# Eight stages on one core: patch work moved between two attentions, gates chosen in four groups, keys and values projected ahead of a norm

## The chip, the cores and the metric

One core of a Trainium2 chip runs the whole kernel. The metric is the device time of one execution in microseconds (us). The engines are PE (TensorE, matmuls), DVE (VectorE), ACT (ScalarE), POOL (GpSimd) and SP (SyncE, which only issues transfers here). They run side by side, each in the order of its own program, and wait for one another by semaphores.

## The reference, cut to what matters

x has 4 batches of 256 rows of 128 (1024 rows). Each stage normalises x and adds its result to it. Four of the eight stages are touched.

```python
x = x + _L0_xattn_ref(...)   # masked attention, 8 heads of 16
x = x + _L0_ffn_ref(...)     # 4 rounds of routed experts
x = x + _L1_xattn_ref(...)   # unmasked attention, 16 heads of 8, context keys too
x = x + _L1_ffn_ref(...)     # gated attention: 8 heads, 8 experts per head
x = x + _L2_xattn_ref(...)   # patch attention
x = x + _L2_ffn_ref(...)     # dense experts
x = x + _L3_xattn_ref(...)   # attention with a null key, 16 heads of 64
x = x + _L3_ffn_ref(...)     # sparse experts

# in _L1_ffn_ref: for values (v) and outputs (o), per row and head, 2 of 8 experts
probs = jax.nn.sigmoid(raw)                       # [B, S, H=8, E=8]
vals, idx = jax.lax.top_k(probs, K)
vals = vals / jnp.clip(vals.sum(-1, keepdims=True), 1e-09) * route_scale
gate = (jax.nn.one_hot(idx, E) * vals[..., None]).sum(-2)

# in _L2_xattn_ref: a decayed running sum over the normalised context, read at boundaries
bidx = jnp.cumsum(patch_lens, axis=1) - 1
boundary_mask = boundary_mask.at[jnp.arange(bsz)[:, None], bidx].set(1)
_, s = jax.lax.associative_scan(comb, (a_b, u), axis=1)
plug = jnp.clip(jnp.cumsum(boundary_mask, axis=1) - 1, 0, plen - 1)
depool_out = depool[jnp.arange(bsz)[:, None], plug]

# in _L3_xattn_ref: queries come from x, keys and values from the context
q = einsum(x, Wq);  k, v = split(einsum(context, Wkv))
k = concatenate((null_k, k));  v = concatenate((null_v, v))
attn = softmax(q * scale @ k.T);  out = layernorm((attn @ v) @ Wout)
```

## The kernel before

Every stage is five Python functions, one per engine, and each engine runs its functions of all stages in a row. x, the normalised `xn`, its transpose `xnT`, the context and its transpose `ctxT` stay in SBUF. The order of work is the order in which the code is written. Between stages the engines are tied by `x_tiles`, a semaphore that DVE raises for each finished tile of x. The `Norm` class makes the norm: statistics on DVE (L80 to L93), a power on POOL (L133), scaling on DVE (L123), eight transposes on PE (L140), and two copies on ACT (L148).

**The attentions (`packed_attention`).** The same function makes stage 0 (masked) and stage 2 (unmasked). Queries and keys are projected, split into three bf16 parts by ACT and DVE (L497, L751, L501, L756), stored to DRAM by SP and ACT (L317) and loaded back in another layout by SP (L652, L662). Then one loop runs over i: a first pass (L365) finds each row's maximum on DVE (L787), the maxima go through a transpose (L422), ACT, DVE or POOL, and a transfer (L721) back into the queries, and some steps later (`LAG`) a second pass (L379), exponentials on ACT (L545) and weighted values (L409) follow. In the masked stage `values` (L351, L774, L778) makes the values of a batch, and the transpose of L422 waits for them.

**The patch work (`PatchAhead`).** The part of patch attention that doesn't depend on x is made early, in the masked attention. The pieces are, in order: `pe_ends`, `dve_hits`, `dve_statistics`, `pe_counts` (L1914), `dve_bounds`, `pe_plugs` (L1927, 8 matmuls), `act_decays` (two Relu L1937, two Exp L1940), `dve_rows` (L1954), `dve_keep` (L1962), `pe_sums` (L1971) and `dve_take` (L1980). Those from `pe_counts` on stand inside the masked loop at i = 0 to 4. PE waits at s = 1 for the last of them (`z_ready`), and POOL waits for it before it splits the weights of the next stage (L1436, L1438).

**The gated attention.** For head h the values are eight experts' products (`experts`, L1554), merged by ACT (L1620), DVE (L1725) and POOL. The gates are chosen by DVE in `select` (L1692 to L1708): 14 operations over rows x heads x experts and 4 narrow ones. It runs four times, each over four heads: side 0 (values) of heads 0 to 3 ahead of everything, side 1 (outputs) of heads 0 to 3 behind the maxima of head 0, and the same for heads 4 to 7 behind the maxima of heads 1 and 2. PE's queries and keys for a head are L1541, the scores L1568, the weighted values L1591; the maxima are L1757.

**The null-key attention.** PE does the transposes of the norm, then the null values times the output weights (L2108), waits until DVE has copied them (L2254), and then projects the first pair of heads in the order q, k, q, k, v, v (L2123, L2126, L2131) through two PSUM banks. Then come the scores (L2148).

## Time and profile before

| | |
|---|---|
| median of 3 runs (lowest, highest) | 1276.37 us (1274.05, 1276.74) |
| the profiled execution: its own time, its span | 1281.73 us, 1280.1 us |
| share of the chain that ended last: PE, DVE, ACT | 68%, 13%, 8% |
| busy: PE, DVE, ACT, POOL | 87%, 61%, 53%, 31% |
| mean granted TensorE clock | 0.908 |
| HBM traffic over the span | 34 GB/s |

The span is counted from the first instruction; 1.6 us of the time lie outside it. The granted clock is a share of 2.4 GHz: 1.00 is 2.4 and 0.50 is 1.2 GHz. By the first and last instruction of each stage the span divides into masked attention 0 to 122 us, rounds to 350, unmasked attention to 523, gated attention to 853, patch attention to 875, dense experts to 1003, null-key attention to 1213, and sparse experts to 1280. PE does most of the chain, but at the start of most stages it is DVE, ACT, POOL and transfers that hold it, and these are the places that the change touches.

### The profile page before, as it was taken

To read this page: it belongs to the slowest core of one execution; us is meant where nothing else is said; L and a number is where in the kernel's file an instruction comes from. 1 tells how busy PE (TensorE), PEld (TensorE's weight loads), DVE (VectorE), ACT (ScalarE), POOL (GpSimd) and SP (SyncE) were. 2 spreads that over 40 slices of the span, in tenths; PEclk is the share of its full clock that TensorE was granted. 3 is DMA by queue.
4 is the path that set the end of the run, shared out by engine and by line. 5 is a ranking of instruction groups with operands and counts; after the bars stand their busy time and mean duration, and the time that the engine had idled before them with its cause. 6 is when DMAs were issued, how large, how long until landed. Compare 5 with 4: busy or idle time off the path is not lost.

```text
span 1280.1 us, 18272 instructions
## 1 busy us (share of the span) xinstructions
PE 1111.4 (87%) x6234; PEld 773.2 (60%) x6234; DVE 781.1 (61%) x1914; ACT 683.4 (53%) x1613; POOL 395.9 (31%) x612
## 2 busy tenths in 40 slices
PE   3677899999859998778899999967999799998777
PEld 2346677777613344656677777745777567675665
DVE  5754687788667672668766677664111366666464
ACT  3253567666515575366677778752343266666022
POOL 5311112111121110236466676672000144444200
PEclk8686899999966799888989999986999899999979
DMA  5411000000050400300000000214000100000000
GB/s 208 100 49 58 1 1 13 1 1 1 1 161 20 170 21 2 132 0 1 1 1 1 1 1 17 116 46 192 1 1 1 67 1 1 1 2 2 1 1 17
DMA packets 26572, 45.10 MB, mean 35 GB/s; under 512 B 3536, under 2 KB 23792, under 8 KB 25200
## 3 DMA queue, kind: packets, MB, share of 16 engines
q1 hardware_dynamic: 23936, 41.57, 9.4%
q10 hardware_dynamic: 2544, 2.36, 0.6%
q8 instruction: 50, 0.82, 0.3%
q14 instruction: 42, 0.34, 0.1%
HBM read 36.94 MB, written 6.82 MB: 34 GB/s over the span
## 4 chain that ended last, share of the span: by engine, by line
PE 68%; DVE 13%; ACT 8%; issue 5%; POOL 2%; DMA 2%; SPq 2%; ACTq 0%; DVEq 0%; POOLq 0%
PE psum L1179 7%; PE psum L1554 7%; PE psum L1169 5%; PE psum L919 5%; PE psum L929 4%; ACT region_d L1620 3%; PE psum L2187 3%; PE psum L409 2%; PE psum L2164 2%; PE psum L2131 2%; PE psum L2148 2%; PE psum L2126 2%; PE psum L1541 2%; PE psum L365 2%; PE psum L1591 2%
## 5 line engine op out<-in xcount | busy, mean ns | idle before, releaser
L1554 PE MATMUL psum<-gated_parts 128*128 128x512 f32 x768 | 198.6, 413 | 16.6 <-DVE region_d L1725 14.7
L1554 PEld LDWEIGHTS psum<-gated_parts 128*128 128x128 f32 x768 | 142.5, 193 | 68.5 <-DVE region_d L1725 32.6
L1794 POOL TENSOR_TENSOR region_d<-region_d 128x256 f32<-128x256 f32 x128 | 101.9, 796 | 121.4 <-DVE region_d L1725 120.1
L1254 ACT ACTIVATE rounds_work<-psum,region_c 128x512 f32<-128x512 f32 x128 | 87.0, 689 | 59.3 <-PE psum L1169 59.2
L787 DVE TENSOR_REDUCE work<-psum 128x1 f32<-128x512 f32 x128 | 82.1, 686 | 34.4 <-PE psum L365 32.8
L1725 DVE SCALAR_TENSOR_TENSOR region_d<-psum,ctx,region_d 128x128 f32<-128x128 f32 x256 | 71.8, 343 | 45.3 <-ACT region_d L1620 41.7
L1620 ACT ACTIVATE region_d<-psum,gated_work 128x128 f32<-128x128 f32 x256 | 75.2, 438 | 44.9 <-issue 26.1
L1179 PE MATMUL psum<-parts,split 128*128 128x512 f32 x384 | 97.6, 404 | 0.0
L1169 PE MATMUL psum<-parts,split 128*128 128x512 f32 x384 | 94.2, 396 | 0.0
L1324 DVE TENSOR_TENSOR parts<-rounds_work,parts 128x1024 fp32r<-128x1024 f32 x64 | 77.5, 1223 | 20.1 <-POOL parts L1410 17.4
L1725 DVE SCALAR_TENSOR_TENSOR region_d<-psum,gated_work,region_d 128x128 f32<-128x128 f32 x256 | 71.3, 344 | 29.1 <-ACT region_d L1620 19.0
L1410 POOL CAST parts<-rounds_work 128x1024 fp32r<-128x1024 f32 x32 | 33.3, 1042 | 179.6 <-ACT rounds_work L1254 179.6
L2215 ACT ACTIVATE null_work<-psum,null_work 128x257 f32<-128x257 f32 x128 | 59.7, 472 | 45.6 <-DVE null_work L2258 45.6
L1169 PEld LDWEIGHTS psum<-parts,split 128*128 128x128 f32 x384 | 73.4, 192 | 15.6 <-issue 0.2
L1179 PEld LDWEIGHTS psum<-parts,split 128*128 128x128 f32 x384 | 70.8, 191 | 19.6 <-issue 6.1
L545 ACT ACTIVATE work<-psum 128x1024 f32<-128x1024 f32 x64 | 65.1, 1024 | 30.5 <-PE psum L379 28.3
L1620 ACT ACTIVATE region_d<-psum,ctx 128x128 f32<-128x128 f32 x256 | 73.7, 385 | 13.8 <-PE psum L1554 12.5
L991 ACT ACTIVATE work_behind<-psum,region_e 128x512 f32<-128x512 f32 x64 | 44.0, 687 | 65.9 <-PE psum L919 64.3
L365 PE MATMUL psum<-work 48*128 48x512 bf16 x128 | 56.3, 481 | 13.6 <-DMA work<-q_parts 10.5
L2258 DVE TENSOR_REDUCE null_work<-psum 128x2 f32<-128x514 f32 x64 | 44.0, 688 | 37.7 <-PE psum L2148 37.7
L1064 DVE SCALAR_TENSOR_TENSOR xn<-psum,work_behind,xn 128x128 f32<-128x128 f32 x64 | 18.0, 344 | 79.9 <-PE psum L929 79.8
L2346 POOL TENSOR_TENSOR null_work<-null_work 128x512 f32<-128x512 f32 x64 | 66.5, 1039 | 0.0
(377 smaller groups left out, 2263.3 us busy)
## 6 DMA issues: line engine op xcount, KB each, us to landing
region_a<-in_l1v SPq DMA_DIRECT2D x1, 4096.0 KB, 15.4
region_b_last<-in_l1o SPq DMA_DIRECT2D x1, 4096.0 KB, 12.4
region_a<-in_l2f SPq DMA_DIRECT2D x1, 4096.0 KB, 13.4
region_b_last<-in_l3f_small SPq DMA_DIRECT2D x1, 4096.0 KB, 19.7
region_a<-in_l3f SPq DMA_DIRECT2D x1, 2080.0 KB, 7.6
region_c<-in_l0f SPq DMA_DIRECT2D x1, 2076.0 KB, 12.3
region_c<-in_l3x SPq DMA_DIRECT2D x1, 2048.0 KB, 8.0
ctx_parts<-front_work SPq DMA_DIRECT2D x6, 256.0 KB, 3.6
```

The lines of the kernel that those rows point to most:

```text
L365: ins = pe.matmul(bank[g % 2][:, j * NK:(j + 1) * NK], QS[b % BUFS][rows_at(side, R_MAX), slot, t * P:(t + 1) * P], KS[b % BUFS][rows_at(s ...
L545: act.activation(PT[s % 2].rearrange("p (a n) -> p a n", a=2), k.pair(2 + 2 * (s % 2)), ACT.Exp, scale=scale).then_inc(p2_exp.semaphore, 1)
L787: dve.tensor_reduce(NM[:, b, heads[0]:heads[0] + HPG, t], bank[g % 2][:, :].rearrange("p (j n) -> p j n", j=HPG), AX.X, ALU.max, negate=Tr ...
L1169: ins = pe.matmul(bank[f], w1_part[a][:, e, f * P:(f + 1) * P], cur_part[b][:, half_of(s % 2)], start=n == 0, stop=n == len(PASSES) - 1)
L1179: ins = pe.matmul(bank[4 + g % 2], w2_part[a][:, g % E, f, :], hidden_part[b][g % 2][:, f, :], start=f == 0 and n == 0, stop=f == FT - 1 a ...
L1254: act.activation(H[g % 2][:, f, :], bank[f], ACT.Gelu_apprx_tanh, bias=W("b1")[:, (g % E) * FT + f:(g % E) * FT + f + 1]).then_inc(h_ready ...
L1324: dve.tensor_tensor(two(hidden_part[1][g % 2], c), two(H[g % 2], c), two(hidden_part[0][g % 2], c).bitcast(F32), ALU.subtract).then_inc(h_ ...
L1554: ins = pe.matmul(bank[2 * (n % 2) + c], src[a][:, t * P:(t + 1) * P], weights[b][:, piece(c)], start=m == 0, stop=m == len(PASSES) - 1)
L1620: ins = act.activation(scaled[n % RING][:, e, :], bank[2 * (n % 2)][:, e * P:(e + 1) * P], ACT.Copy, scale=scalars[:, n % NT, e:e + 1])
L1725: ins = dve.scalar_tensor_tensor(out=tile, in0=bank[2 * (n % 2) + 1][:, e * P:(e + 1) * P], scalar=scalars[:, n % NT, HALF_E + e:HALF_E + ...
L1794: pool.tensor_tensor(tile[:, 0:2, :], tile[:, 0:2, :], tile[:, 2:4, :], ALU.add).then_inc(k.pool_chain, 1)
L2346: pool.tensor_tensor(PR[g % 4][:, :, 0:S], PR[g % 4][:, :, 0:S], r.broadcast_to([P, TPB, S]), ALU.mult)\
```

## The change

Four edits. (1) `pe_plugs`, `act_decays`, `dve_rows`, `dve_keep`, `pe_sums` and `dve_take` leave the masked attention for the front of the unmasked one; `pe_counts` and `dve_bounds` stay in the masked stage, ahead of its loop. What the late pieces need (`upto16`, `before`, `least`, `bound`) lies in a new SBUF tensor, `patch_kept`. (2) POOL's split of the next stage's weights waits for the first exponential instead of `z_ready`. (3) `select` runs eight times, over head groups of 1, 3, 2 and 2. (4) In the null-key attention the first pair's chunks go in the order k, k, v, v, q, q, three of them ahead of the norm's transposes and in banks of their own, and L2108 comes last.

```diff
@@ packed_attention, tensor @@
         if masked:
             ahead.pe_ends(pe)
+        else:
+            pe.wait_ge(k.x_tiles, NT * number)
+            ahead.pe_plugs(pe)
         k.norm.tensor(pe, use, k.xn)
...
         if masked:
             pe.wait_ge(*biased.at(4))
+            ahead.pe_counts(pe)
         else:
             pe.wait_ge(*rest.at(first_of(3)))
             pe.wait_ge(*part.at(first_of(3)))
+            ahead.pe_sums(pe)
...
-                if masked and s == 1:
-                    pe.wait_ge(ahead.z_ready, 2)
+                if s == 1:
+                    pe.wait_ge(*((ahead.bound_ready, 1) if masked else (ahead.z_ready, 2)))
...
-            if masked and i == 0:
-                ahead.pe_counts(pe)
-            if masked and i == 1:
-                ahead.pe_plugs(pe)
-            if masked and i == 3:
-                ahead.pe_sums(pe)
@@ scalar, gpsimd, vector @@
+        if not masked:
+            ahead.act_decays(act)
         k.norm.scalar(act, use, k.xnT)
...
-            if masked and i == 1:
-                ahead.act_decays(act)
...
-            pool.wait_ge(ahead.z_ready, 2)
+            pool.wait_ge(*p2_exp.at(1))
             split.gpsimd(pool)
...
+            if pair == 0 and not masked:
+                ahead.dve_rows(dve, chain)
+                ahead.dve_keep(dve)
         if masked:
             ahead.dve_hits(dve, chain)
             ahead.dve_statistics(dve, chain)
+            ahead.dve_bounds(dve)
+        else:
+            ahead.dve_take(dve)
@@ gated_attention @@
+    GATE_GROUPS = (slice(0, 1), slice(1, 4), slice(4, 6), slice(6, 8))
...
-                if h % (NH // 2) == 0:
-                    act.wait_ge(gates_ready, 1 if h == 0 else 3)
+                for i, heads in enumerate(GATE_GROUPS):
+                    if h == heads.start:
+                        act.wait_ge(gates_ready, 2 * i + 1)
...
             if h < NH:
+                if h == 1:
+                    select(2)
+                elif 1 < h < 6:
+                    select(h + 2)
                 merge_block(values_block(h), gates[:, :, 0, h, :])
                 if h > 0:
                     maxima(h)
                 if h == 0:
-                    select(1, first_heads)
-                elif h < 3:
-                    select(h - 1, last_heads)
+                    select(1)
+                elif h == 1:
+                    select(3)
@@ null_key_attention @@
+    FIRST = (1, 3, 4, 5, 0, 2)
...
+    def chunk(p, i):
+
+        n, c = len(CHUNKS) * p + i, FIRST[i] if p == 0 else i
+        return n, c, c // 2 % 2 if c < 4 else c - 4, k.bank[1 + i] if n < 2 else k.bank[6 + n % 2]
...
-        for c in range(len(CHUNKS)):
-            project(0, c)
+        for i in range(3):
+            project(0, i)
+        k.norm.tensor(pe, use, k.xn, banks=(4, 5))
+        project(0, 3)
+        for i in range(4, 6):
+            pe.wait_ge(k.norm.T_ready, 2 * use + i - 3)
+            project(0, i)
+        for p in range(PAIRS):
+            ins = pe.matmul(bank[5][0:HEADS, 0:D], W("nv")[:, p, :], W("o")[:, p, :], start=p == 0, stop=p == PAIRS - 1)
+        ins.then_inc(nvw_psum, 1)
         pe.wait_ge(null_ready, 4)
         scores(0, 0)
+        pe.wait_ge(nvw_sb, 1)
```

Three places of the order, before and after. ACT at the front of the unmasked attention, before (`parts` and `rounds_work` belong to the stage ahead):

```order
L1265 ACTIVATE rounds_work<-psum 128x512 x2
L148 ACTIVATE xnT<-psum 128x512 x2
L497 ACTIVATE work<-psum 128x512 x2
L501 ACTIVATE work<-work 128x512 x2
L317 DMA q_parts<-work 16x8x512 x6
```

The same place on ACT after the change:

```order
L1265 ACTIVATE rounds_work<-psum 128x512 x2
L1945 ACTIVATE work<-psum,patch_kept 128x1024 x2
L1948 ACT_TABLE_LOAD
L1948 ACTIVATE work<-work 128x1024 x2
L148 ACTIVATE xnT<-psum 128x512 x2
L500 ACTIVATE work<-psum 128x512 x2
L504 ACTIVATE work<-work 128x512 x2
L319 DMA q_parts<-work 16x8x512 x6
```

Two Relu and two Exp of 1024 columns stand ahead of the copies of the transposes, and the load of the Exp table, which stood at L545 behind the first maxima, is now among them. DVE at the same front after the change:

```order
L752 TENSOR_TENSOR work<-psum,work 128x512 x2
L757 TENSOR_TENSOR work<-work 128x512 x2
L1960 TENSOR_SCALAR ctx_rstd<-ctx_rstd 128x8
L1962 SCALAR_TENSOR_TENSOR work<-ctx,ctx_rstd,region_e 128x128 x8
L1970 SCALAR_TENSOR_TENSOR work<-psum,patch_kept,work 128x1024 x2
L752 TENSOR_TENSOR work<-psum,work 128x512 x2
L757 TENSOR_TENSOR work<-work 128x512 x2
L1988 TENSOR_TENSOR mask_bc<-psum,region_e 128x512 x2
```

The two halves of the splitting, which stood side by side, now have 11 instructions between them. PE at the front of the null-key attention, before:

```order
L929 MATMUL psum<-region_a,work_behind 128x128 x32
L140 MATMUL psum<-ident,xn 128x128 x8
L2108 MATMUL psum<-region_d 16x128 x8
L2123 MATMUL psum<-xnT,region_d 128x512
L2126 MATMUL psum<-ctxT,region_c 128x512 x2
L2123 MATMUL psum<-xnT,region_d 128x512
L2126 MATMUL psum<-ctxT,region_c 128x512 x2
L2131 MATMUL psum<-region_c,ctxT 128x128 x16
L2148 MATMUL psum<-null_parts 128x258 x24
```

And after:

```order
L929 MATMUL psum<-region_a,work_behind 128x128 x32
L2138 MATMUL psum<-ctxT,region_c 128x512 x4
L2143 MATMUL psum<-region_c,ctxT 128x128 x8
L140 MATMUL psum<-ident,xn 128x128 x8
L2143 MATMUL psum<-region_c,ctxT 128x128 x8
L2135 MATMUL psum<-xnT,region_d 128x512 x2
L2188 MATMUL psum<-region_d 16x128 x8
L2160 MATMUL psum<-null_parts 128x258 x24
```

Both keys and half of the values stand between the last matmuls of the stage ahead and the transposes, and only one half of the values, the queries and the null values are left behind them.

## Rows read from the trace of the kernel before

**Rows 1.** Timeline, masked attention: start us, us, instruction, [idle before <- releaser].
```profile
37.08 2.19 DVE L1954 SCALAR_TENSOR_TENSOR front_work<-ctx,ctx_rstd,region_e 128x128 f32<-128x128 f32 x8
...
39.30 2.12 ACT L1937 ACTIVATE front_work<-psum,front_work 128x1024 f32<-128x1024 f32 x2 [12.22 <-PE psum L1927]
...
43.70 2.45 DVE L1962 SCALAR_TENSOR_TENSOR front_work<-psum,front_work 128x1024 f32<-128x1024 f32 x2
...
44.89 21.62 SPq L721 DMA_DIRECT2D front_work<-front_work  x10
...
46.20 5.22 PE L1971 MATMUL psum<-front_work 128*128 128x128 f32 x32 [3.48 <-DVE front_work L1962]
...
55.53 2.41 POOL L1438 TENSOR_TENSOR split<-region_c,split 128x1024 fp32r<-128x1024 f32 x1
...
56.11 2.90 DVE L778 TENSOR_SCALAR front_work<-front_work,mask_col 128x128 f32<-128x128 f32 x2
...
59.16 0.27 PE L422 MATMUL psum<-ident,front_work 128*8 128x128 f32 x1 [3.76 <-DVE front_work L778]
...
71.09 0.48 DVE L778 TENSOR_SCALAR front_work<-front_work,mask_col 128x128 f32<-128x128 f32 x2
...
93.32 2.08 PE L351 MATMUL psum<-region_d,ctxT 128*128 128x128 f32 x8
```

**Rows 2.** Timeline, front of the unmasked attention.
```profile
354.27 0.60 ACT L148 ACTIVATE xnT<-psum 128x512 f32<-128x512 f32 x1 [9.82 <-PE psum L140]
...
363.62 1.29 DVE L751 TENSOR_TENSOR work<-psum,work 128x512 f32<-128x512 f32 x2 [3.19 <-ACT work L497]
...
369.90 0.61 PE L365 MATMUL psum<-work 48*128 48x512 bf16 x2 [10.50 <-DMA work<-q_parts]
...
388.28 1.28 ACT L545 ACT_TABLE_LOAD   x1
389.57 1.94 ACT L545 ACTIVATE work<-psum 128x1024 f32<-128x1024 f32 x2
```

**Rows 3.** Windows: stretch, us, busy (instructions) by engine, granted clock, DMA.
```profile
388.00:394.00 6.00, 5.43 (x37) 1.78 (x35) 3.87 (x6) 4.51 (x5) 0.00 (x0) 0.50 0.00 0
```

**Rows 4.** Timeline of PE and DVE, gated attention.
```profile
537.03 3.72 PE L1568 MATMUL psum<-gated_work 128*128 128x256 f32 x16 [0.69 <-ACT gated_work L1647]
...
565.53 6.58 PE L1541 MATMUL psum<-xnT,region_d 128*128 128x512 f32 x8 [3.47 <-DVE gated_parts L1741]
...
609.04 3.72 PE L1591 MATMUL psum<-region_c,gated_work 128*128 128x256 f32 x16
...
653.20 3.71 PE L1591 MATMUL psum<-region_c,gated_work 128*128 128x256 f32 x16
...
689.93 3.72 PE L1591 MATMUL psum<-region_c,gated_work 128*128 128x256 f32 x16
...
556.55 0.41 DVE L1692 TENSOR_REDUCE gated_work<-ctx 128x32 f32<-128x256 f32 x1
...
564.92 0.22 DVE L1749 TENSOR_TENSOR gated_work<-ctx,gated_work 128x64 f32<-128x64 f32 x1
...
574.09 1.13 DVE L1725 SCALAR_TENSOR_TENSOR region_d<-psum,ctx,region_d 128x128 f32<-128x128 f32 x4 [7.62 <-ACT region_d L1620]
...
662.33 1.12 DVE L1725 SCALAR_TENSOR_TENSOR region_d<-psum,ctx,region_d 128x128 f32<-128x128 f32 x4 [4.53 <-ACT region_d L1620]
```

**Rows 5.** Timeline of PE, front of the null-key attention.
```profile
1007.06 2.50 PE L140 MATMUL psum<-ident,xn 128*128 128x128 f32 x8 [5.71 <-DVE xn L123]
...
1009.49 2.98 PE L2108 MATMUL psum<-region_d 128*16 128x128 f32 x16
...
1012.93 1.10 PE L2123 MATMUL psum<-xnT,region_d 128*128 128x512 f32 x2 [0.46 <-DVE null_work L2254]
...
1019.04 3.73 PE L2131 MATMUL psum<-region_c,ctxT 128*128 128x128 f32 x32
...
1022.70 0.98 PE L2148 MATMUL psum<-null_parts 64*128 64x258 f32 x12
```

More of the change, by code:

```diff
@@ L218, in packed_attention @@
         cp = [k.carve(BF16, T) for _ in range(3)]
+    else:
+        ahead.carve_later()
     q_dram, k_dram = k.q_dram[number], k.k_dram[number]
@@ L795, in vector @@
                     row_maxima(b, n)
-            if masked and i == 0:
-                ahead.dve_bounds(dve)
-                ahead.dve_rows(dve, chain)
             if masked and i % SU == 0 and 0 < i <= ALL:
@@ L810, in vector @@
                                   ALU.subtract).then_inc(nm_rest.semaphore, 1)
-            if masked and i == 2:
-                ahead.dve_keep(dve)
-            if masked and i == 4:
-                ahead.dve_take(dve)
             if masked and i % STEPS == VALUES_AT % STEPS and VALUES_AT <= i < ALL + VALUES_AT:
@@ L1679, in vector, with select @@
         dve.wait_ge(probs_ready, 1)
-        shape = [P, NT, NH // 2, E]
-        falling = W("falling").unsqueeze(1).unsqueeze(1).broadcast_to(shape)
-        def wide(a):
-            return a.unsqueeze(3).broadcast_to(shape)
-        def select(side, heads):
+        def select(n):
+            side, heads = n % 2, GATE_GROUPS[n // 2]
+            shape = [P, NT, heads.stop - heads.start, E]
+            falling = W("falling").unsqueeze(1).unsqueeze(1).broadcast_to(shape)
+            wide = lambda a: a.unsqueeze(3).broadcast_to(shape)
             of = lambda a: a.rearrange("p (t a h) e -> p t a h e", t=NT, a=2)[:, :, side, heads, :]
@@ L1708, in select @@
             dve.tensor_tensor(g, g, wide(c2), ALU.mult).then_inc(gates_ready, 1)
-            dve.wait_ge(gates_ready, side + 2 * (heads.start > 0) + 1)
+            dve.wait_ge(gates_ready, n + 1)
         def low_weights(n, c):
@@ L2229, in projections @@
             ins.then_inc(proj_sb, 1)
-        for c in range(len(CHUNKS)):
-            projections(0, c)
+        for i in range(3):
+            projections(0, i)
+        k.norm.scalar(act, use, k.xnT, banks=(4, 5))
+        for i in range(3, 6):
+            projections(0, i)
         exponentials(0)
```

75 lines of the change are left out of this document (36 added, 39 removed).

## The prediction

> **What bounds the kernel now.** I read the chain that ended last first: PE holds 68% of it. In the middle of every stage PE is full, and a change on another engine is worth nothing there. So I looked, stage by stage, at the first microseconds on the timeline: what stands idle, and whose end it waits for. The four edits touch four such fronts, and I cost each at the instruction of PE or DVE behind which the rest of the stage follows as before.
>
> **Masked attention: what leaves.** In the rows of the loop, PE waits 3.48 us for DVE's L1962, computes the sums for 5.22 us, and reaches the maxima's transpose L422 at 59.16, 3.76 us late, released by DVE's L778 [rows 1]. Leaving are 2.19 us (L1954) and 2.45 us (L1962) on DVE, two pairs of 2.1 us on ACT (L1937 and its Exp), and 5.22 us on PE. Their sum, 14 us, is not the gain, because SP bounds this front too: the first transfer of maxima is issued at 44.89 [rows 1], behind the loads of all batches, and that doesn't move. Three issues and the flight of the last take some 3.6 us (estimate), so the second pass starts at 48.5. Then PE does the second pass, a first pass and the values. It has done little by then and its clock will be low, where the values took 2.08 us [rows 1]; with the passes, 3.3 us, to 51.8. DVE adds the bias (0.4) and runs L778. Before, L778 took 2.90 us with POOL's L1438 of 2.41 us beside it, and 0.48 us once POOL was done [rows 1]. POOL's split now starts after the first exponential, at about 50.5, so it meets L778 again, and I take 2.90 us: 55.1 against 59.16, **-4.0 us**. If L778 escapes it is -6.5; if one more such meeting occurs later, -2. Behind this the loop runs at its old pace. The counts, now ahead of the loop, lie in PE's wait for the loaded queries.
> The 2.4 us that L778 lost fit what the Trainium skill says in "SBUF — State Buffer", on the shared port: DVE and GpSimd lock one port pair for a whole instruction and the second one blocks. By that rule moving POOL's start to the first exponential keeps the collision, which is the case I took; without the rule I would say -6.5.
>
> **Unmasked attention: what comes in.** The plugs fit PE's pause before the transposes and cost nothing; they are ready at about 350.8. ACT then does the Relu pair (2.12 [rows 1]), the table load (1.28 [rows 2]) and the Exp pair (2.0, taken as the Relu pair), to 356.1, where its L148 began at 354.27 [rows 2]: 1.8 us late. All behind it (projection, splitting, q stores, loads) shifts by this, since PE's L365 ends a wait of 10.50 us for the loaded queries at 369.90 [rows 2]; it would start at 371.7. DVE has a pause of 3.19 us ahead of L751 at 363.62 [rows 2], from 360.4, now 362.2. Into it go rows and keep: 2.4 + 2.5 = 4.9 us, to 367.0, then the subtractions L751 (1.3) to 368.3. PE waits for these before the sums; the 5.22 us of the sums [rows 1], again after a long pause, end at 373.5. That is 3.6 us later than 369.90. Back comes the table load of L545 at 388.28 [rows 2], of which I count 0.3, because PE had other work nearly to its end. `dve_take` waits for the sums and delays the first maxima by about 0.1. POOL's fills and the second half of the stores have several us to spare. **+3.3 us.** Bounds: +1.8, if the sums run at the full clock in 3.4 and end before the queries land; +5, if PE starts the projections slower by the low clock as well.
> The Trainium skill ("ScalarE: Activation LUTs", What ACT_TABLE_LOAD costs) adds a drain of about 1.38 us to each load. The trace shows none: the load at 388.28 ends with its 1.28 us and the next ACTIVATE starts at 389.57 [rows 2]. By the page the term would be +4.7, and the total 1260.7.
>
> **Gated attention.** A select over four heads costs 7.5 us: 14 wide operations of 0.41 with a gap of 0.04, and about 1.1 for the narrow ones (from 556.55 to 564.92 it stood 8.4, with a reciprocal and two stretched operations in it) [rows 4]. An operation on 64 columns takes 0.22 [rows 4]. So one head costs 14 x 0.26 + 0.95 = 4.5 us; by interpolation three heads cost 6.5 and two heads 5.5. DVE's total grows from 30 to 44 us, and the place decides.
> - Ahead of head 0 the select ends 3 us earlier, but PE's scores end at 540.75 [rows 4] and the first merge waits for ACT behind them: 0, at most -0.3.
> - Behind head 0: 4.5 in place of 8.1, and PE continues at 562.1 instead of 565.53, up to -3.5 and a warm L1541 in place of 6.58 us [rows 4]. But head 1 waits for its own select: DVE is free at 563.3, ends three heads at 569.8, and ACT starts there instead of just ahead of the merge of 574.09, at 572.85: **-3.0**. PE stands 2.7 us meanwhile; a low clock after this costs up to 2 more. I take +1.
> - Behind the maxima of head 1: 6.5 instead of 7.5, **-1.0**.
> - Head 2 had the last select. From L1591 to L1591 it took 44.16 us, and head 3 took 36.73 [rows 4]: **-7.4**.
> - Heads 2 to 5 now begin with a select of 5.5 in DVE's pause of 4.53 [rows 4]: merges 0.9 late. PE is two tiles ahead of DVE and DVE merges faster than PE multiplies, so PE loses about 0.5 each: **+2**. Bounds 0 and 3.7.
> Together -8.4, taken as **-8.5 us**; from -12 to -5.
>
> **Null-key attention.** PE is idle for 5.71 us before the transposes at 1007.06 [rows 5], from 1001.35. Two keys (each twice a query's 1.10, less when warm) and half of the values (1.9 of the 3.73) [rows 5] fill it nearly: 5.3 to 6.3 us. The last tile of xn sets the end of the transposes, 1009.3. After it come the other half of the values (1.8), two queries (0.9 each) and L2108: 2.98 before [rows 5], half on a low clock, now 1.7 to 2.9. Scores start at 1014.6 to 1015.8 instead of 1022.70 [rows 5]; q's low part is ready at about 1013.4. PE has been busy since 1001, so I take 1014.8: **-7.9 us**; from -9 to -6.
>
> **The sum.** -4.0 + 3.3 - 8.5 - 7.9 = -17.1 us. The profiled execution took 1281.7 (span 1280.1 and 1.6 around it) and would take 1264.6. It is 5.4 above the median of the runs, and none of the four places depends on that, so the forecast is 1276.4 - 17.1 = **1259.3 us**.
>
> **Rivals.**
> - *The sums keep PE warm* in the unmasked stage. From 388 to 394 PE was busy 5.43 of 6 us at a granted clock of 0.50 [rows 3], and stayed so for some eight steps of 2 us. If the 5 us of full matmuls raise the clock and it lasts over 17 us of first passes, these steps end on DVE at about 1.5 us: -3.7 more, 1255.6. For it: after the sums in the masked stage the clock was full. Against: it fell there at the next pause of PE.
> - *The gates bite.* Every late merge costs its full 0.9 us and head 1 leaves PE cold: +1.7 and +1, with the low bound of the masked stage about +2: 1264.
> - *The table switch drains*: 1260.7, as above.
> - *Slower*: PE's pause in heads 1 to 5 is long enough for the clock to fall. L1541 took 6.58 us after 3.47 us of idling [rows 4] and half as much when warm, so each head would cost 3.3 + 0.9. Five of them are 21 us against the 3 in my sum: +18, 1277. It decides from 3.9 us per head on. Against it: the select exceeds the pause by 0.9 us only, and PE kept its clock over its pauses of that length.
> - *The early projections do nothing*, because another engine holds the scores: DVE's low parts or POOL's null keys. Both are done by 1013.4 in my count. If wrong, up to +5, 1264.
>
> **How the numbers follow.** All four terms within their bounds near the middle 0.55; warm sums 0.15; gates or other terms at their weak ends 0.17; the drain 0.05; slower 0.03; something unseen 0.05. The forecast is that of the first. The bounds added in squares give about 5 us down and 5 up; with warm sums below and the weak ends above I give 1250 to 1268. A change below 0.2% (2.6 us) can hardly be measured. Faster by more 0.95, within 0.02, slower 0.03.
>
> **What would show it.** In the new trace: the second pass of the masked stage at 48 to 49 and the first L422 behind the values near 55; L778 again at 2.9; stage 2 starting 4 us earlier; its first L370 3.6 us later from the end of stage 1 than before, behind the sums; ACT's table load at L1948; head 1's first scaling behind the end of a select; head 2 near 37 us instead of 44; no pause of PE ahead of the null-key transposes; 12.5 to 14 us from the last L929 to the first scores, where it was 21.3. I am wrong if pauses of PE and a clock of 0.50 appear at the start of heads 2 to 5, or if the unmasked front grows by more than 5 us.

## The result, and the profile of the changed kernel

| | median us (lowest to highest) | executions | ratio of times, 95% |
|---|---|---|---|
| before | 1276.08 (1273.69 to 1279.12) | 16 | |
| changed | 1269.53 (1263.85 to 1283.76) | 16 | 0.9946 (0.9923 to 0.9969) |

The change made the kernel 6.9 us faster (0.0054 x 1276). The prediction was 1259.3 with a range to 1268, so it was 10 us too low, and the result lies outside the range. The changed kernel's executions also spread over 20 us where those of before spread over 5, and follow the mean granted clock: at 0.919 they took 1264 to 1267, at 0.912 and less 1270 and more. The ratios, here and below, leave out an execution that lies more than 1.5% above the fastest of its kernel (1283.76 here), which the medians keep.

The table shows where the time went, stage by stage, in the two profiled executions (1281.73 and 1275.16 us, each some 5.5 us above the median of its kernel). The ends of the stages are read from first and last starts: PE's first L464 (L465 now), the last matmul of the rounds at L1179, DVE's first L123 of the gated attention and of its successor, L123 of the null-key stage, PE's first L2460 (L2482).

| stage | predicted | before, us | changed, us | difference |
|---|---|---|---|---|
| masked attention | -4.0 | 106.6 | 106.9 | +0.3 |
| rounds | 0 | 239.8 | 238.3 | -1.5 |
| unmasked attention | +3.3 | 176.2 | 184.1 | +7.9 |
| gated attention | -8.5 | 339.2 | 332.0 | -7.2 |
| up to the null-key norm | 0 | 144.9 | 145.4 | +0.5 |
| null-key attention | -7.9 | 211.2 | 204.6 | -6.6 |
| last stages | 0 | 62.2 | 62.2 | 0 |

The two later stages did nearly what was forecast; the two attentions between which the patch work moved did not. First the masked one, timeline of the changed kernel (start us, us, instruction, [idle before <- releaser]); it answers to [rows 1]:
```profile
46.96 42.68 SPq L722 DMA_DIRECT2D front_work<-front_work  x21
...
54.68 1.03 PE L384 MATMUL psum<-front_work 100*128 100x256 bf16 x4 [8.84 <-DMA front_work<-front_work]
...
57.96 2.34 POOL L1438 TENSOR_TENSOR split<-region_c,split 128x1024 fp32r<-128x1024 f32 x1
58.39 2.97 DVE L785 TENSOR_SCALAR front_work<-front_work,mask_col 128x128 f32<-128x128 f32 x2
...
61.51 0.37 PE L427 MATMUL psum<-ident,front_work 128*8 128x128 f32 x1 [3.23 <-DVE front_work L785]
```
The work of the patch attention is gone, yet the transpose behind the values starts at 61.51, later than the 59.16 of [rows 1]. PE stood 8.84 us for a DMA. The prediction had the first transfer of maxima issued at 44.89 as before and the second pass at 48.5; it was issued at 46.96 and the second pass came at 54.68, 7.7 us behind the issue where the prediction had 3.6. L785 beside POOL's split took 2.97 us, as foreseen.

The front of the unmasked attention, which answers to [rows 2]:
```profile
348.67 1.05 PE L1935 MATMUL psum<-patch_kept 128*128 128x256 bf16 x8 [0.85 <-DVE x L1366]
...
349.75 2.12 ACT L1945 ACTIVATE work<-psum,patch_kept 128x1024 f32<-128x1024 f32 x2 [6.51 <-PE psum L1935]
...
351.89 1.28 ACT L1948 ACT_TABLE_LOAD   x1
353.19 2.00 ACT L1948 ACTIVATE work<-work 128x1024 f32<-128x1024 f32 x2
...
355.82 2.04 PE L347 MATMUL psum<-xnT,region_d 128*128 128x512 f32 x2 [1.50 <-ACT xnT L148]
...
362.43 2.19 DVE L1962 SCALAR_TENSOR_TENSOR work<-ctx,ctx_rstd,region_e 128x128 f32<-128x128 f32 x8
364.54 2.46 DVE L1970 SCALAR_TENSOR_TENSOR work<-psum,patch_kept,work 128x1024 f32<-128x1024 f32 x2
366.92 1.27 DVE L752 TENSOR_TENSOR work<-psum,work 128x512 f32<-128x512 f32 x2
...
368.25 6.35 PE L1979 MATMUL psum<-work 128*128 128x128 f32 x32 [6.75 <-DVE work L752]
...
374.53 0.39 PE L370 MATMUL psum<-work 48*128 48x512 bf16 x2
...
377.17 1.20 PE L370 MATMUL psum<-work 48*128 48x512 bf16 x2 [0.21 <-DVE work L794]
```
The order of events is the predicted one: decays on ACT, rows and products on DVE, then the sums, which took 6.35 us for the 5.22 of [rows 1], and the first pass directly behind them.

The gated attention, PE, which answers to [rows 4]. Between the copies of L1592 lie heads 2 and 3:
```profile
569.26 3.70 PE L1542 MATMUL psum<-xnT,region_d 128*128 128x512 f32 x8 [0.39 <-DVE gated_parts L1741]
...
612.84 3.72 PE L1592 MATMUL psum<-region_c,gated_work 128*128 128x256 f32 x16
...
650.32 3.71 PE L1592 MATMUL psum<-region_c,gated_work 128*128 128x256 f32 x16
...
687.75 3.72 PE L1592 MATMUL psum<-region_c,gated_work 128*128 128x256 f32 x16
```
Head 2 takes 37.48 us (44.16 before) and head 3 37.43 (36.73 before). The matmuls of L1542, those of queries and keys, took 3.70 us where they took 6.58.

The front of the null-key attention, PE, which answers to [rows 5]:
```profile
1007.05 1.09 PE L140 MATMUL psum<-ident,xn 128*128 128x128 f32 x4 [0.49 <-DVE xn L123]
1008.30 1.10 PE L140 MATMUL psum<-ident,xn 128*128 128x128 f32 x4 [0.16 <-DVE xn L123]
1009.24 1.95 PE L2143 MATMUL psum<-region_c,ctxT 128*128 128x128 f32 x16
1011.02 2.04 PE L2135 MATMUL psum<-xnT,region_d 128*128 128x512 f32 x4
1012.99 1.92 PE L2188 MATMUL psum<-region_d 128*16 128x128 f32 x16
1014.84 0.98 PE L2160 MATMUL psum<-null_parts 64*128 64x258 f32 x12
1018.67 1.66 PE L2160 MATMUL psum<-null_parts 64*128 64x258 f32 x12 [2.84 <-ACT null_work L2235]
```
The pause of 5.71 us is filled, and the scores start at 1014.84 where the prediction said 1014.8.

### The profile page after: what moved, and what is told of

Its sections match the earlier page's. It is cut to its first block, busy times and chain, and to the rows that moved or that the text cites. A ratio compares the mean times of both kernels' runs of the same rounds, so it can differ in the third digit from the quotient of the medians.

```text
span 1273.5 us, 18344 instructions
## 1 busy us (share of the span) xinstructions
PE 1113.0 (87%) x6234; PEld 772.5 (61%) x6234; DVE 787.3 (62%) x1986; ACT 684.2 (54%) x1613; POOL 395.4 (31%) x612
## 4 chain that ended last, share of the span: by engine, by line
PE 66%; DVE 11%; ACT 9%; issue 5%; SPq 3%; DMA 2%; POOL 2%; ACTq 0%; DVEq 0%; POOLq 0%
PE psum L1179 8%; PE psum L1169 7%; PE psum L1555 6%; PE psum L919 5%; PE psum L929 4%; ACT region_d L1621 4%; PE psum L2208 3%; PE psum L2176 2%; PE psum L2160 2%; PE psum L414 2%; PE psum L2143 2%; ACT region_c L1638 2%; PE psum L1592 2%; PE psum L1569 2%; PE psum L2138 2%
## 5 line engine op out<-in xcount | busy, mean ns | idle before, releaser
L1179 PE MATMUL psum<-parts,split 128*128 128x512 f32 x384 | 99.3, 408 | 0.0
L1169 PE MATMUL psum<-parts,split 128*128 128x512 f32 x384 | 96.7, 402 | 0.0
L1621 ACT ACTIVATE region_d<-psum,ctx 128x128 f32<-128x128 f32 x256 | 73.5, 383 | 20.5 <-PE psum L1555 16.4
L1179 PEld LDWEIGHTS psum<-parts,split 128*128 128x128 f32 x384 | 70.8, 191 | 20.9 <-issue 6.1
L548 ACT ACTIVATE work<-psum 128x1024 f32<-128x1024 f32 x64 | 65.2, 1024 | 34.0 <-PE psum L384 31.9
L929 PEld LDWEIGHTS psum<-region_a,work_behind 128*128 128x128 f32 x512 | 59.5, 192 | 7.2 <-issue 7.2
```

The costliest lines, as they stand in the source:

```text
L548: act.activation(PT[s % 2].rearrange("p (a n) -> p a n", a=2), k.pair(2 + 2 * (s % 2)), ACT.Exp, scale=scale).then_inc(p2_exp.semaphore, 1)
L929: ins = pe.matmul(bank[4 + g % 2][:, t * P:(t + 1) * P], H[g % 2][:, f, t * P:(t + 1) * P], W("w2")[:, i // 2, f, :], start=f == 0, stop=f ...
L1169: ins = pe.matmul(bank[f], w1_part[a][:, e, f * P:(f + 1) * P], cur_part[b][:, half_of(s % 2)], start=n == 0, stop=n == len(PASSES) - 1)
L1179: ins = pe.matmul(bank[4 + g % 2], w2_part[a][:, g % E, f, :], hidden_part[b][g % 2][:, f, :], start=f == 0 and n == 0, stop=f == FT - 1 a ...
L1621: ins = act.activation(scaled[n % RING][:, e, :], bank[2 * (n % 2)][:, e * P:(e + 1) * P], ACT.Copy, scale=scalars[:, n % NT, e:e + 1])
```

## The experiments

### One part at a time

Theory at this point: the missing 10 us belong to the patch move, by some mechanism in the two attentions. Rival: the three parts act on each other. The three parts touch different functions, so each was put alone on the kernel before. Runs e1, e2, e3 and e4, in this order; the edits are the parts of the diff above (e1: `packed_attention`, `PatchAhead` and the memory lines; e2: `gated_attention`; e3: `null_key_attention`; e4: the last two).

> The patch attention's move alone, gates and null-key attention as before. By the steps of the prediction this would be -4.0 in the masked attention and +3.3 in the unmasked one, -0.7 us, so about 1275.4. By the profile of the changed kernel (masked attention +0.3, rounds -1.4, unmasked attention +8.0) it is about +7 us, 1283. Which of the two comes shows whether the missing 10 us of the forecast all belong to this part. A second theory, that the missing time lies in the join of the three parts (gates or null-key stage slowed by the moved memory), wants about 1276 here.

> The gates in four groups alone. Predicted -8.5 us, so 1267.6; the profile of the changed kernel shows -7.2 in that stage, so 1268.9 if the edits don't act on each other. If the parts do act on each other, this one differs from -7.2 by more than 1 us.

> The null-key attention's keys and values ahead of the norm alone. Predicted -7.9 us, so 1268.2; the profile of the changed kernel shows -6.5, so 1269.6.

> Gates and null-key edits, the patch attention left where it was. If the three parts add up and the patch move costs about 7 us: -13.7 by the changed kernel's profile, 1262.4, faster than the changed kernel. If the patch move is worth -0.7 as predicted and the loss is an interaction, this one has about the changed kernel's time, 1270. The spread over executions is looked at too: the changed kernel's runs lie 20 us apart and those of the kernel before 5 us; if the patch move brought the spread, this kernel's runs lie within some 6 us.

| | median us | ratio to before, 95% | as a difference |
|---|---|---|---|
| e1 patch move | 1280.84 | 1.0046 (1.0024 to 1.0068) | +5.9 |
| e2 gates | 1270.15 | 0.9957 (0.9942 to 0.9973) | -5.5 |
| e3 null-key | 1272.77 | 0.9972 (0.996 to 0.9984) | -3.6 |
| e4 gates and null-key | 1264.28 | 0.9907 (0.989 to 0.9925) | -11.9 |

The patch move alone makes the kernel slower by 5.9 us, near the +7 that the profile gave and far from the -0.7 of my sum; without it the kernel is 5 us faster than with it. The gates and the null-key edit alone measure less than in their stages, and together more than their sum. The profiles say where they lose when alone. In e2 the null-key attention, whose code is that of before, took 213.7 us for 211.2: behind a wait of the same length the twelve matmuls of the scores took 1.66 us (e2, first line) where before (second line) took 0.99, and within the next 6 us PE fell 2.5 us behind.
```profile
1013.22 1.66 PE L2152 MATMUL psum<-null_parts 64*128 64x258 f32 x12 [2.75 <-ACT null_work L2219]
```
```profile
1026.43 0.99 PE L2148 MATMUL psum<-null_parts 64*128 64x258 f32 x12 [2.75 <-ACT null_work L2215]
```
In e3 that stage took 207.3 us where e4's took 204.6. The difference arises late, over a stretch of the same work in both: the granted clock was 0.59 from 1172 to 1180 in e3 and 1.00 from 1167 to 1175 in e4. It is one profile of each kernel, so this places the loss in these executions and does not tell how often it comes.

The spread seemed to follow the patch move, since e4's executions lie within 5.2 us and e1's within 14.7. Later runs don't bear that out: e6 and e12, without the move, spread over 16.4 and 14.6 us, and e7, with it, over 4.7.

### What is slow in the masked attention: a start address

The transfer queue of SP, before:
```profile
41.47 1.46 SPq L662 DMA_DIRECT2D front_work<-k_parts  x3
42.98 1.87 SPq L662 DMA_DIRECT2D front_work<-q_parts  x4
```
and changed:
```profile
41.10 3.04 SPq L663 DMA_DIRECT2D front_work<-k_parts  x3
44.18 2.73 SPq L663 DMA_DIRECT2D front_work<-q_parts  x4
```
The same seven loads took 3.3 us of SP before and 5.8 after. The view of the DMA queues over the first 60 us (packets, MB, share of 16 engines) says why. Before:
```profile
q1 hardware_dynamic: 8720, 9.05, 51.9%
```
Changed:
```profile
q1 hardware_dynamic: 8720, 9.05, 65.4%
```
The same packets and bytes took longer, 57 ns for one (0.519 x 60 us x 16 / 8720) against 72. It was 66.6% in e1 and 53.6 to 54.4% in e2, e3 and e4, so it belongs to the patch move. The move adds a tensor `patch_kept` of 264 words ahead of the work area, which so begins 1056 bytes further on. The area holds the slots to which the loads write rows of 256 bf16 numbers, 512 bytes. Theory A: the new start address makes the packets slow. Theory B: what the engines do beside the loads. Four kernels shift nothing but that address.

e5, e7: the changed kernel with 8 and 24 words more (1088 and 1152 bytes).
```
-PATCH_KEPT = S + 2 * TPB + NT // 2
+PATCH_KEPT = S + 2 * TPB + NT // 2 + 8      # e7: + 24
```
e6, e8: the kernel before with an unused tensor of 8 and 32 words (32 and 128 bytes).
```
         self.mask_bias = sb("mask_bias", [1, T], BF16)
+        self.pad = sb("pad", [P, 8])            # e8: 32
...
-WORK = REGION_B + 18090
+WORK = REGION_B + 18090 - 8                     # e8: 32
```


> The changed kernel with 8 words more in the new tensor of kept values, 272 instead of 264, so that the work area behind it starts 1088 bytes later than in the kernel before instead of 1056; nothing else. In both kernels that hold the patch move the DMA packets of the first 60 us take 65 to 67% of the window against 52 to 54% in the four without it, same packets and bytes. Theory A, the shift of the work area by 1056 bytes (32 bytes off a multiple of 64) makes the packets slow: here the share is back to 52 to 54%, the first transfer of maxima is issued at about 43.5 and lands as before, the masked attention ends 2 to 4 us earlier than the changed kernel's 106.9, and the time falls by about 3 us to 1266.5. Theory B, the missing POOL, ACT and DVE work beside the loads or the changed order makes them slow: share 65 to 67% again, 1269.5. The Trainium skill, page DMA: Bandwidth & Descriptors, section How a descriptor splits into AXI transactions, counts from multiples of 256 bytes, and by it this shift would bring nothing.

> The kernel before with an unused tensor of 8 words (32 bytes) ahead of the work area, which is 8 words shorter; not one instruction differs. Theory A: the packets of the first 60 us take about 66%, the masked attention ends some 2 us later (about 107.5), and the time is 2 to 4 us above 1275.9. Theory B: 52 to 54% and no difference.

> The changed kernel with 24 words more in the kept tensor, so that the work area lies 1152 bytes later than before, on a multiple of 256 by my addition of the tensors ahead of it. Theory A: as with 8 words more, 1266.5. If multiples of 256 bytes count, as the same section of the Trainium skill has it, this one is better than the one with 8 words more and its packets take less than 52%.

> The kernel before with an unused tensor of 32 words (128 bytes) ahead of the work area. Theory A: no difference to before (52 to 54%, 1276). If multiples of 256 count: packets below 52% and a gain of 1 to 3 us.

The unused 32 bytes of e6 raised the share from 52 to 65.3%, without one instruction changed, so theory B falls. But so did 128 bytes (e8, 63.1%), and e5 and e7 stayed at 61.1 and 62.3%: so it is not multiples of 64, as I had it in theory A. The times are: e5 1265.50 (0.9891, 0.9857 to 0.9925), e7 1265.40 (0.9903, 0.9877 to 0.9929), e6 1278.35 (1.0007, 0.9984 to 1.003), e8 1279.09 (1.001, 0.9994 to 1.0026). To the kernel before the slow packets cost nothing that can be measured, which refutes the 2 to 4 us that I expected.

In the built program the work area of the kernel before starts at byte 123136, 481 x 256, and none of the shifts so far keeps a multiple of 256; e7 and e8 had been meant as such multiples, by a wrong sum of the tensors ahead of the area. The next four are these: e9 is the changed kernel with `+ 56` (1280 bytes, 5 x 256), e12 the kernel before with an unused tensor of 64 words, and e10 and e11 ask about the unmasked attention on the layout of e9. e10 keeps of the patch attention's late pieces nothing but the bias; its edit, with `dve_take` as in e18 below:
```
-            ahead.pe_plugs(pe)
-            ahead.pe_sums(pe)
-            ahead.act_decays(act)
-                ahead.dve_rows(dve, chain)
-                ahead.dve_keep(dve)
```
e11 puts all but the rows into the unmasked loop; of its edit, the lines added there (those ahead of the loop go):
```
+            if not masked and i == 0:
+                ahead.pe_plugs(pe)
+            if not masked and i == 4:
+                ahead.pe_sums(pe)
...
+            if not masked and i == 0:
+                ahead.act_decays(act)
...
+            if not masked and i == 2:
+                ahead.dve_keep(dve)
+            if not masked and i == 6:
+                ahead.dve_take(dve)
```


> The changed kernel with 56 words more in the kept tensor (320 words), so that the work area starts 1280 bytes later than before. By the allocation in the built programs the area starts at byte 123136 in the kernel before, which is a multiple of 256; the shifts tried so far (32, 128, 1056, 1088 and 1152 bytes) all leave that, and in all of them the packets of the first 60 us take 61 to 67% instead of 52 to 54%. Theory A2 (in place of multiples of 64): rows of 512 bytes that start off a multiple of 256 are slow; here the share is 52 to 54% and the first transfer of maxima is issued at 43.5 or earlier, and the masked attention ends at about 103 (some 2 us below the 104.2 to 106.6 of the kernels without the patch move). Time about 1264, against 1269.5. Theory B, the share depends on what the engines do beside the loads: 61% or more again. This is what the Trainium skill says (DMA: Bandwidth & Descriptors, How a descriptor splits into AXI transactions).

> The kernel before with an unused tensor of 64 words (256 bytes) ahead of the work area. Theory A2: no difference from before, packet share 52 to 54%, where 32 and 128 bytes gave 65 and 63%. If any shift does harm: 61% or more.

e9 took 1263.62, ratio 0.9872 (0.984 to 0.9904), against 0.9946 (0.9923 to 0.9969) for the changed kernel: the two intervals don't meet. By the whole time the case for the address is weaker than this pair makes it, though. The other kernels off the multiple measure 0.9891 (e5), 0.9903 (e7) and, below, 0.9918 (e17), and each of their intervals meets e9's; so does that of e4 (0.989 to 0.9925). What shows the address is the masked attention itself. e9's packets:
```profile
q1 hardware_dynamic: 8736, 9.05, 52.9%
```
and its masked attention:
```profile
42.57 19.89 SPq L722 DMA_DIRECT2D front_work<-front_work  x10
47.55 1.03 PE L384 MATMUL psum<-front_work 100*128 100x256 bf16 x4 [5.43 <-DMA front_work<-front_work]
...
51.26 2.97 DVE L785 TENSOR_SCALAR front_work<-front_work,mask_col 128x128 f32<-128x128 f32 x2
...
54.37 0.37 PE L427 MATMUL psum<-ident,front_work 128*8 128x128 f32 x1 [3.23 <-DVE front_work L785]
```
The second pass came at 47.55 and the transpose at 54.37, where the prediction had 48.5 and 55.1, and the stage ends at 101.0. So the prediction's chain for this stage holds on a layout that the change did not keep. Its two times came out partly by luck: from issue to second pass it took 5.0 us for the 3.6 of the working, and the issue at 42.57 in place of 44.89 made up for it (4.2 to 5.0 us and issues at 42.57 to 43.92 in e9, e10, e11 and e18).

e12 (1278.74, 0.9999, 0.9973 to 1.0025) did not fit: on a multiple of 256 its share read 59.8%. Runs e13 to e16 ask about that, with one execution each: the changed kernel, the kernel before and e12 again without any edit, and the kernel before with an unused tensor of 256 words (1024 bytes).

> The changed kernel once more, unchanged. If the layout sets the packets' time: 65 to 67% of the first 60 us again. If it is a matter of each loading of the program: it can come out at 52 to 54%.

> The kernel before once more, unchanged. Layout: 52 to 54% again. Each loading: can be 60% or more.

> The kernel before with the unused 256 bytes, once more. Layout by a rule other than multiples of 256: about 60% again. Each loading: can be 52 to 54%. A reading of 52 to 54% here with 65% and 52% in the two beside it would leave multiples of 256 as the rule and the first reading as an exception.

> The kernel before with an unused tensor of 256 words (1024 bytes) ahead of the work area, which so starts again at 256 bytes behind a multiple of 512 (and of 1024), as in the kernel before. Multiples of 256, or a rule of 512 or 1024 bytes: 52 to 54%. If only the exact old place and 1280 bytes are good by chance: 60% or more.

They read 63.6% (e13), 54.3% (e14), 50.0% (e15) and 54.5% (e16). So the first reading of e12's kernel was the exception. Last, e17 takes e9 off its multiple again, by 32 bytes (`+ 64` in place of `+ 56`).

> The changed kernel with 328 kept words: 8 words (32 bytes) more than the one with 320 that was the fastest, not one instruction different. Layout theory: packets of the first 60 us from 52.9% to some 65%, the masked attention's end from 101.0 to about 107, and the time from 1263.6 to about 1268. Theory that the packets depend on each loading: no difference in the mean.

Its share is 63.6%, its masked attention ends at 106.5, and its time is 1266.30, ratio 0.9918 (0.9898 to 0.9938). The table has all profiles, by where the work area starts:

| work area starts | kernels | packets' share, first 60 us | end of the masked attention |
|---|---|---|---|
| multiple of 256, patch work in the masked stage | before, e2, e3, e4, e12, e14, e15, e16 | 50.0 to 54.5%, once 59.8% | 104.1 to 106.6, mean 105.4 |
| multiple of 256, patch work moved or left out | e9, e10, e11, e18 | 51.7 to 53.3% | 99.2 to 101.2, mean 100.3 |
| off it, patch work in the masked stage | e6, e8 | 65.3, 63.1% | 105.2, 106.5 |
| off it, patch work moved | changed, e1, e5, e7, e13, e17 | 61.1 to 66.6% | 106.5 to 109.5, mean 107.7 |

By the ends of the stage, the move gains 5.1 us on a multiple of 256 (105.4 to 100.3) and loses 1.9 off it (105.8 to 107.7), 2.3 against the kernels of the first row. The address costs 0.5 us, within the scatter, while the patch work stands in the stage, since PE has the sums to do while the maxima travel, and 7.4 us when it is gone. The move took away the cover under which the slower transfer was free, and made the transfer slower, in one edit.

Counted by size in the traces, it is the loads that get slower. The 6176 packets of 512 bytes in the first 60 us are the rows that the loads write into the area. They took 36 to 43 ns each in the mean in eleven of the twelve profiles on a multiple of 256 (50.5 in e12), and 53 to 60 ns in the eight off it. The 1536 packets of 1024 bytes are the rows that the stores read out of the same area, and they took 50.5 to 54.5 ns on a multiple and 51.3 to 54.3 off it.

The Trainium skill ("DMA: Bandwidth & Descriptors", How a descriptor splits into AXI transactions) has a descriptor cut at multiples of 256 bytes, and one that starts off such a multiple fetches the bytes ahead of its start for nothing. If the same held for the side that is written, a row of 512 bytes would be two transactions on a multiple of 256 and three off it, and the trace agrees as to where the border lies. As to the side it does not agree: the page tells of bytes that are read, and the stores, which by that rule would make five transactions out of four, got no slower. Counted in beats of 32 bytes, as the page does, it would be 16 on a multiple, 17 for a start 32 bytes past one and 20 for 128 bytes past; the trace shows 63.6 to 66.6% for 32 bytes past and 62.3 and 63.1% for 128, so beats don't fit. Three transactions in place of two is an inference, and how the written rows get slower stays open.

### What the unmasked attention pays

> The kernel with 320 kept words, and the plugs, decays, rows, products and sums of the patch attention left out altogether: its term is the bias alone, so the output is not the reference's. It gives what the masked attention gains without any price in the unmasked one. The prediction's step says the unmasked stage pays 3.3 us; the profiles say that the first pass starts 5 us later (374.5 against 369.3 to 369.9). So by the first this kernel is 3.3 us below the one with 320 words, by the second 5 to 6 us.

> The kernel with 320 kept words, but in the unmasked attention only the rows u stay ahead of the first pass; plugs behind its step 0, decays on ACT at step 0, the products with the gaps at step 2, the sums at step 4 and the last addition at step 6. Theory C, the price in the front is the ACT work ahead of the transposed copies plus sums at the low clock ahead of the first pass: this kernel pays only some 4 us of DVE work (2 products, 2 additions) in a phase that DVE sets, so 1 to 2 us below the kernel with 320 words. Theory D, wherever it stands it costs its whole length in a phase of row maxima and low clock: no difference.

> The kernel with 320 kept words, with plugs, decays, rows and products as they are, but without the 32 matmuls of the sums (PE waits for the products at the same place, the term is the bias alone, so the output is not the reference's). The kernel without any of it was 4.6 us faster than the one with 320 words. If the sums on PE are the price: this one is as fast as that, ratio 0.983 to 0.985. If the ACT and DVE work ahead of the projections is the price: no difference from 0.987.

The edit of e18, on e9:
```
-            ahead.pe_sums(pe)
+            pe.wait_ge(ahead.kept, TPB)
...
-            dve.tensor_tensor(self.z[:, 4 * h:4 * h + 4, :], self.k.bank[4 + h].rearrange("p (t d) -> p t d", t=4),
-                              self.W("b").unsqueeze(1).broadcast_to([P, 4, P]), ALU.add).then_inc(self.z_ready, 1)
+            dve.tensor_copy(self.z[:, 4 * h:4 * h + 4, :],
+                            self.W("b").unsqueeze(1).broadcast_to([P, 4, P])).then_inc(self.z_ready, 1)
```
The first passes and second passes of the table count from the last matmul of the rounds.

| | median us | ratio, 95% | first pass, us | second pass, us | stage, us |
|---|---|---|---|---|---|
| patch work not here (10 profiles) | | | 23.4 to 23.9 | 41.4 to 41.9 | 169.2 to 176.2, mean 171.4 |
| e10, nothing | 1256.02 | 0.9836 (0.9806 to 0.9865) | 23.6 | 41.6 | 172.9 |
| e18, all but the sums | 1266.74 | 0.9905 (0.9882 to 0.9927) | 26.1 | 44.9 | 176.1 |
| e9, all, in the front | 1263.62 | 0.9872 (0.984 to 0.9904) | 29.3 | 46.7 | 179.1 |
| all 7 with it in the front | | | 29.3 to 29.5 | 46.7 to 47.3 | 173.9 to 184.1, mean 179.0 |
| e11, in the loop | 1274.17 | 0.9965 (0.9942 to 0.9987) | 23.9 | 53.3 | 189.8 |

The front agrees within 0.5 us in all profiles of a kind: the move delays the first pass by 5.7 us, of which 2.5 are there without the sums and 3.2 are theirs. By time e9 lies 4.6 us above e10 (0.0036 x 1278), a little under the 5 to 6 us expected; the two intervals overlap slightly, so this is a size and not a proof. e18 did not come out as either theory had it: its front is 3.2 us earlier than e9's and its time is not shorter, ratio 0.9905 against 0.9872 with intervals that overlap. Its two copies of the bias took 2.44 us of DVE just where the first maxima were due (the same copies in e10 fell into a pause of DVE), and its executions show clocks of 0.906 to 0.916 where e9's show mostly 0.914 to 0.924. What these two cost was not tested. So the sums' price in the front is shown and their price in the whole is not.

e11 is 10.5 us worse than e9 by the medians, and neither theory C nor theory D had that. Theory C counted 4 us of DVE work and overlooked PE:
```profile
373.91 2.67 DVE L791 TENSOR_REDUCE work<-psum 128x1 f32<-128x512 f32 x4
...
375.79 6.65 PE L1980 MATMUL psum<-work 128*128 128x128 f32 x32
382.36 0.10 PEld L367 LDWEIGHTS psum<-work 48*128 48x128 bf16 x2
382.37 0.39 PE L367 MATMUL psum<-work 48*128 48x512 bf16 x2
382.79 2.48 DVE L791 TENSOR_REDUCE work<-psum 128x1 f32<-128x512 f32 x4 [6.21 <-PE psum L367]
```
DVE, which sets the pace of the first pass, stands 6.21 us while PE does the sums. And the clock came back late. The windows of e11 (stretch, length, busy us by PE, PEld, DVE, ACT, POOL, granted clock, DMA share, GB/s):
```profile
400.00:410.00 10.00, 10.00 (x66) 3.49 (x61) 5.48 (x9) 4.74 (x6) 1.40 (x4) 0.50 0.01 1
410.00:420.00 10.00, 10.00 (x71) 3.67 (x69) 6.22 (x10) 5.40 (x6) 0.00 (x0) 0.50 0.22 61
```
and of e9:
```profile
400.00:410.00 10.00, 9.99 (x105) 3.67 (x102) 8.77 (x14) 7.42 (x9) 0.60 (x2) 1.00 0.21 61
410.00:420.00 10.00, 9.91 (x102) 4.45 (x101) 7.72 (x14) 7.25 (x10) 1.31 (x5) 1.00 0.56 211
```
PE is full in both and does two thirds of the matmuls in e11, at the lower level (0.50 is 1.2 of 2.4 GHz).

The rest of the 7.6 us of the stage (179.0 - 171.4), some 2 us, I put down to the clock too, without a run that shows it; it is what scatters. The stage's code is the same in before and e4, and they differ by 3.5 us. Windows of 445 to 465 in before, in the changed kernel and in e4:
```profile
445.00:465.00 20.00, 19.90 (x175) 8.45 (x179) 14.18 (x24) 12.68 (x16) 1.40 (x4) 0.83 0.11 31
```
```profile
445.00:465.00 20.00, 20.00 (x149) 7.67 (x141) 12.19 (x21) 11.25 (x14) 1.91 (x6) 0.65 0.11 31
```
```profile
445.00:465.00 20.00, 19.90 (x199) 8.13 (x200) 16.65 (x27) 14.98 (x19) 1.40 (x4) 1.00 0.12 32
```
A PE that is full at 0.65 does 149 matmuls where it does 199 at 1.00.

## Why the prediction was wrong, point by point

- **Masked attention, forecast -4.0, measured +0.3 in the profiled pair, and +2.3 as a mean over the kernels with such an address: the step that failed.** It said that the first transfer of maxima "is issued at 44.89 [rows 1], behind the loads of all batches, and that doesn't move", and took 3.6 us from there to the second pass, a figure for which no row of before stands. In the changed kernel it was issued at 46.96 and PE went on 7.7 us later, at 54.68. Shown by e6, e9 and e17: the tensor of kept values moves the work area off a multiple of 256 bytes, and its loads get slower. The diff showed the new tensor, and I costed it at nothing. With the address mended the step measured -5.1, inside its bounds, with both of its times within 1 us, though an earlier issue and a longer flight made up for each other in them.
- **L778 against POOL**: 2.90 taken, 2.97 measured in the changed kernel and in e9. This was right, and the trace agrees with the rule of the Trainium skill that I had weighed ("SBUF — State Buffer", Who interferes with whom).
- **Rounds, 0**: this was right; over all profiles they took 239.7 to 241.5 without the patch move and 238.1 to 241.5 with it.
- **Unmasked attention, forecast +3.3, measured +7.9 in the pair and +7.6 as a mean: the term that was mis-sized.** Each event is there. The first pass came 5.7 us later where the working had 3.6: the sums began 23.0 us behind the rounds' last matmul where the working had 21.9 (PE started the projections at the lower clock, 2.04 us for the first two of L347, the reason of my upper bound), and they took 6.35 where I took 5.22 from [rows 1]. That is 1.1 us each. The other 2 us come behind the front and were not in the sum.
- **Gated attention, forecast -8.5, measured -7.2** (e2 alone -7.1 in its stage). Up to head 2 it gave -2.95, forecast -3.0 (-3.0, +1 and -1.0). Head 2: -6.7, forecast -7.4 and 0.5 of the +2. Heads 3 to 5: +0.7 to +0.9 each, forecast +0.5 and bounded by 0.9. It was right in mechanism and 1.3 too large, most of it in the late merges. The slower rival, a clock that falls in the pauses of heads 2 to 5, did not come: L1592 keeps its 3.71 to 3.72 us.
- **Null-key attention, forecast -7.9, measured -6.6.** The scores came at 1014.84, as said. Then PE waits 2.84 us for ACT, as it waited 2.75 before, and the twelve matmuls behind the wait take 1.66 us where they took 0.99, at the lower clock. At the next projection the lead is 6.6. The -7.9 was that of the first scores, and I did not follow it to the second. Why the clock fell in this wait and not in the equally long one before is not settled; e2 shows the same fall behind the same 2.75 us in the order of before. The rival that the early projections do nothing is false.
- **The table load**: 1.28 us, the next ACTIVATE 0.02 us behind it. There was no drain, as [rows 2] had it, which is other than the Trainium skill says ("ScalarE: Activation LUTs", What ACT_TABLE_LOAD costs); the measurement decides.
- **Warm sums**: this rival is false. PE leaves the sums at the high clock (0.99 from 374.5 to 377.0), and from 377.0 to 380.0 the granted clock is 0.50.
- **The sum.** On the mended address the changed kernel measures 0.9872, which is 1260.1 on the forecast's base of 1276.4, against the forecast 1259.3. That is no merit of the sum: by the profiles its terms are there -5.1, +7.6, -7.2 to -10.0 and -6.6, together -11 to -14, and the ratio's interval is -12 to -20 us. All four terms were off by more than 1 us, the unmasked one by 4.3, and not all the same way.

Shown are: that the patch move costs 5.9 us by itself; that the start address slows the rows that the loads write; that in the masked attention this eats the gain of the move; and the 5.7 us in the unmasked front and their parts. Argued only are: three transactions in place of two; and that the clock's return makes the last 2 us. Open are: why the clock fell in the null-key attention of e2 and late in that of e3, which is where the two later edits, singly 9.1 us and together 11.9, lose; what sets the spread of a kernel's executions; and why leaving the sums out won no time.

## What to carry to other kernels

One profile of a stage is not its time: here the same stage differed by 7 us between profiles, so compare several before a difference is explained. A new small tensor is not free because it is small: ask what lies behind it, and keep areas to which DMAs write short rows (512 bytes here) on multiples of 256 bytes. Before work is moved out of a stage, look for the transfer that it covered, and cost that transfer at its worst, since it becomes the wait. Work put in front of a phase cost its own length on the path (5.7 us); put into a phase that another engine paces, it stopped that engine too and cost most (e11).

## What the hardware showed that was not expected

- The same 8720 packets took 50.0 to 54.5% of the first 60 us (once 59.8%) with the work area on a multiple of 256 bytes, and 61 to 67% off it, an unused tensor of 32 bytes being enough (e6). Rows of 512 bytes written into the area took 36 to 43 ns on and 53 to 60 ns off it; rows of 1024 bytes read out of it took the same.
- The reading of one kernel can stray: it was 59.8 and 50.0% for the same kernel in e12 and e15.
- Behind the same wait of 2.75 us the same twelve matmuls took 0.99 us in one kernel (before) and 1.66 in another (e2), and the stage then took 2.5 us longer.
- An identical stage lasted from 169.2 to 176.2 us in ten profiles, while its front agreed to 0.5 us; where the profiles were compared, the granted clock went back to full at different times.
